# Target scores in fp32r, the x half of the output projection per group, destinations written by GpSimd, late gathers on two queues

## The reference, cut to what matters

```
q = (LN(x) @ Wtgt.T + b) * mask;  k, v = split((ctx @ Wsrc.T + b) * mask)     # 8 heads of 16
a = softmax(q @ k.T / 4, masked keys out) @ v
x = x + tanh(g0) * (concat[LN(x), a] @ Wout.T + b)          # Wout: 256 -> 128
p = softmax(LN(x) @ router.T);  two best of 8 experts, weights made to sum to 1
x = x + tanh(g1) * sum over the two of  w * (gelu(LN(x) @ w1[e]) @ w2[e])
```

## Time and profile before

| engine | busy us | share of the span | instructions |
|---|---|---|---|
| PE | 297.5 | 88% | 3633 |
| DVE | 212.3 | 63% | 905 |
| ACT | 189.1 | 56% | 470 |
| POOL | 205.9 | 61% | 274 |

### The profile page before, as it was taken

The page is one execution under the profiler, slowest core; times in us unless marked ns, Lnnn a source line. Parts: engine busy times, 40 slices in busy tenths (PEclk is TensorE's granted clock), DMA queues, the critical chain, the costliest instruction groups (busy, mean ns, idle before and its releaser), DMA issues.

```text
span 339.5 us, 10975 instructions
## 1 busy us (share of the span) xinstructions
PE 297.5 (88%) x3633; PEld 267.0 (79%) x3633; DVE 212.3 (63%) x905; ACT 189.1 (56%) x470; POOL 205.9 (61%) x274
## 2 busy tenths in 40 slices
PE   1989999999999999997989979999998999999500
PEld 1777777787877878785678969999998999999500
DVE  2457567679888887889677866338733343437720
ACT  3166758868696876767674437456444444444100
POOL 3433233243586867858367787878878865567821
PEclk9999999999999999999999989999999999999955
DMA  6524521213141211851244222211434432194451
GB/s 221 158 86 167 166 85 33 80 37 95 33 123 53 64 50 49 243 143 33 59 105 118 63 68 83 68 52 61 126 91 128 114 105 64 39 317 139 143 171 46
DMA packets 41236, 34.61 MB, mean 102 GB/s; under 512 B 5044, under 2 KB 36950, under 8 KB 41184
## 3 DMA queue, kind: packets, MB, share of 16 engines
q1 hardware_dynamic: 33152, 23.62, 24.6%
q0 software_dynamic: 4320, 8.47, 7.0%
q10 hardware_dynamic: 3712, 1.84, 1.9%
HBM read 22.35 MB, written 12.01 MB: 101 GB/s over the span
## 4 chain that ended last, share of the span: by engine, by line
PE 47%; POOL 21%; issue 13%; DVE 8%; ACT 4%; DMA 3%; SPq 1%; POOLq 0%; ACTq 0%; DVEq 0%
POOL rows L638 10%; PE ps_sc L1572 8%; POOL picked L656 8%; PE ps_o L1531 4%; PE ps_proj L1585 4%; PE ps_o L1585 4%; PE ps_proj L1460 3%; PE ps_proj L1463 3%; PE ps_sc L1413 3%; PE ps_sc L1425 3%; PE ps_sc L1408 2%; PE ps_xT L1454 2%; DVE rowmax L1205 2%; ACT xr L787 2%; POOL pscratch L651 2%
## 5 line engine op out<-in xcount | busy, mean ns | idle before, releaser
L656 POOL DMA_INDIRECT picked<-yo,xg x71 | 71.5, 1007 | 16.1 <-issue 11.1
L1572 PE MATMUL ps_sc<-xt,w1c 128*128 128x128 f32 x568 | 76.2, 278 | 3.2 <-issue 2.4
L638 POOL DMA_INDIRECT rows<-xr,posi x64 | 63.2, 987 | 18.0 <-issue 18.0
L1572 PEld LDWEIGHTS ps_sc<-xt,w1c 128*128 128x128 f32 x568 | 69.8, 194 | 4.3 <-issue 4.3
L821 ACT ACTIVATE probT<-ps_sc 128x512 f32<-128x512 f32 x71 | 42.4, 598 | 43.6 <-PE ps_sc L1572 43.6
L1205 DVE TENSOR_REDUCE rowmax<-ps_sc 128x4 f32<-128x512 f32 x64 | 43.7, 691 | 24.7 <-PE ps_sc L1429 20.6
L716 ACT ACTIVATE probT<-ps_sc,pencol 128x512 f32<-128x512 f32 x64 | 43.6, 683 | 20.5 <-PE ps_sc L1429 18.3
L586 POOL TENSOR_TENSOR kblk<-kT,headcol 128x256 f32<-128x256 f32 x32 | 19.7, 615 | 54.3 <-ACT kT L745 54.1
L1585 PE MATMUL ps_proj<-w2s,probT 128*128 x288 | 38.9, 279 | 0.0
L1585 PE MATMUL ps_o<-w2s,probT 128*128 x280 | 37.1, 275 | 0.0
L1323 DVE COPY w1c<-w1s 128x512 f32 x71 | 31.6, 449 | 7.1 <-PE ps_sc L1572 2.3
(11 more groups left out here) (166 smaller groups left out, 585.5 us busy)
## 6 DMA issues: line engine op xcount, KB each, us to landing
xg<-rows SPq DMA_DIRECT2D x71, 65.0 KB, 1.9
ctxs<-ctxT SPq DMA_DIRECT2D x32, 128.0 KB, 2.1
xs<-x SPq DMA_DIRECT2D x8, 256.0 KB, 3.3
maskbc<-mask SPq DMA_DIRECT2D x8, 256.0 KB, 4.0
w1s<-w SPq DMA_DIRECT2D x4, 512.0 KB, 3.6
w2s<-w SPq DMA_DIRECT2D x8, 256.0 KB
maskbc<-picked SPq DMA_DIRECT2D x4, 512.0 KB, 6.0
out<-xs ACTq DMA_DIRECT2D x6, 256.0 KB, 2.3
```

The costliest lines, as they stand in the source:

```text
L638: nc.gpsimd.indirect_dma_start(out=rows, out_offset=bass.IndirectOffsetOnAxis(ap=posi[:, i, pick, b:b + 1], axis=0), in_=xr[:, i, pick, b, ...
L656: nc.gpsimd.indirect_dma_start(out=picked, out_offset=bass.IndirectOffsetOnAxis(ap=xg[:, r, D + 1:D + 2].bitcast(I32), axis=0), in_=yo[:, ...
L1572: last = nc.tensor.matmul(ps_score[j % DEEP][:, c * 128:(c + 1) * 128], w1c[:, j % DEEP, c * 128:(c + 1) * 128], xt[:, j % XRING, :], star ...
```

## The change

- The target scores take fp32r operands: GpSimd makes a second product `kblkr`, ahead of `kblk`, and ScalarE a copy `qTr` of qT; TensorE waits for these, and for `kblk` only in the part of sequence m.
- The x half of the output projection leaves the step. `xnT` becomes a ring of 12, and at (G+3, 1) the group's four x halves are accumulated in `ps_tail` with the attention halves. DVE's add of the x half and `s_xo` go.
- 16 bf16 matmuls on a tile of ones at the start of TensorE's stream; DVE sets this tile first.
- GpSimd writes the destinations into `xr`, behind its waits for the group's scatter, and waits for its own write.
- Of the last seven sends the last two are again a pair.
- The late gathers 1 and 3 are issued by ScalarE, 0 and 2 by SyncE; both wait for the last 20 sends in the order of the slots; all late adds are DVE's.

```diff
@@ -60,6 +60,7 @@
 DEEP = 3
+WARM = 16
@@ -73,10 +74,12 @@
 KQ = 4
+XNRING = 3 * GROUP
 BOXES = 3
...
 SINGLY = SLOTS - 7
+LAST_PAIR = SLOTS - 2
@@ -218,10 +221,12 @@
         xn = sb("xn", [128, GROUP, D])
-        xnT = sb("xnT", [128, 2, T])
+        xnT = sb("xnT", [128, XNRING, T])
         kT = sb("kT", [128, KQ, T])
...
         kblk = sb("kblk", [128, KQ, PAIR, T])
+        kblkr = sb("kblkr", [128, KQ, PAIR, T], F32R)
+        qTr = sb("qTr", [128, KQ, T], F32R)
         spare = sb("spare", [128, 3 * GROUP * 2 * D])
@@ -409,11 +416,9 @@
-        ROUTE = 23
+        ROUTE = 22
@@ -556,13 +561,14 @@
-            for r in range(RING):
-                sp.wait_ge(f_send[r], 16 * len(range(r, SLOTS, RING)))
+            for j in range(SLOTS - RING, SLOTS):
+                sp.wait_ge(f_send[j % RING], 16 * (j // RING + 1))
             for i, (G, half) in enumerate(LATE):
-                sp.dma_start(yb[G][:, half], picked_v[:, late(G, half), :, :]).then_inc(s_late_yb[i], 16)
+                if not i % 2:
+                    sp.dma_start(yb[G][:, half], picked_v[:, late(G, half), :, :]).then_inc(s_late_yb[i], 16)
             for i, (G, half) in enumerate(LATE):
                 if i % 2:
-                    sp.wait_ge(s_pool_y2, i // 2 + 1)
+                    sp.wait_ge(s_late_y2, i + 1)
                     sp.dma_start(out_v[:, late(G, half), :], xs[:, late(G, half), :]).then_inc(s_out, 16)
@@ -583,6 +589,9 @@
                     wait(pool, s_sc, n - 2)
+                    nc.gpsimd.tensor_tensor(
+                        kblkr[:, r, :, :], kT[:, r, :].unsqueeze(1).broadcast_to([128, PAIR, T]),
+                        headcol[:, :].unsqueeze(2).broadcast_to([128, PAIR, T]), ALU.mult).then_inc(s_kblkr, 1)
                     nc.gpsimd.tensor_tensor(
@@ -632,6 +641,10 @@
                     pool.wait_ge(s_xr, G + 1)
+                    nc.gpsimd.tensor_copy(
+                        xr[:, i, :, :, D + 1].bitcast(I32),
+                        dest[:, bass.ds(GROUP * G, GROUP), :].rearrange("p b k -> p k b")).then_inc(s_label, 1)
+                    pool.wait_ge(s_label, G + 1)
                     settled()
@@ -665,23 +678,16 @@
                 j = slot_of(n, LAG_DOWN)
-                if j is not None and (j % 2 or j >= SINGLY):
+                if j is not None and (j % 2 if j < SINGLY else j != LAST_PAIR):
                     pool.wait_ge(f_y, j + 1)
-                    wait(pool, f_settled, j // 2 if j < SINGLY else SINGLY // 2 + j - SINGLY)
+                    wait(pool, f_settled, j // 2 if j < SINGLY else SINGLY // 2 + min(j, LAST_PAIR) - SINGLY)
                     settled().then_inc(f_settled, 1)
-                    if j < SINGLY:
+                    if j < SINGLY or j > LAST_PAIR:
                         send(j - 1)
...
             each_slot(step, slot)
-            for i, (G, half) in enumerate(LATE):
-                if i % 2:
-                    x2 = xs[:, late(G, half), :]
-                    pool.wait_ge(s_late_yb[i], 16)
-                    nc.gpsimd.tensor_tensor(x2, x2, yb[G][:, half, 0, :], ALU.add).then_inc(s_pool_y1, 1)
-                    pool.wait_ge(s_pool_y1, i // 2 + 1)
-                    nc.gpsimd.tensor_tensor(x2, x2, yb[G][:, half, 1, :], ALU.add).then_inc(s_pool_y2, 1)
@@ -722,8 +728,8 @@
                     act.wait_ge(s_xT, n + 1)
-                    wait(act, s_proj, n - 1)
-                    nc.scalar.activation(xnT[:, (k - LAG_PROJ) % 2, :], ps_xT[:, 0:T],
+                    wait(act, s_oproj, n // GROUP - 2)
+                    nc.scalar.activation(xnT[:, n % XNRING, :], ps_xT[:, 0:T],
                                          ACT.Copy).then_inc(s_xnT, 1)
@@ -732,6 +738,11 @@
                     exponent(n, FAR, far_heads, s_exp)
+                n = sequence(g, k, LAG_SCORE)
+                if n is not None:
+                    act.wait_ge(s_q, n + 1)
+                    wait(act, s_sc, n - 3)
+                    nc.scalar.activation(qTr[:, n % KQ, :], qT[:, n % KQ, :], ACT.Copy).then_inc(s_qr, 1)
                 G = group(g, LAG_ROUTE)
@@ -741,6 +752,7 @@
                     act.wait_ge(s_proj, n + 1)
+                    wait(act, s_kblkr, n - 3)
                     wait(act, s_kblk, n - 3)
@@ -829,9 +841,14 @@
                 store(G)
+            for j in range(SLOTS - RING, SLOTS):
+                act.wait_ge(f_send[j % RING], 16 * (j // RING + 1))
+            for i, (G, half) in enumerate(LATE):
+                if i % 2:
+                    act.dma_start(yb[G][:, half], picked_v[:, late(G, half), :, :]).then_inc(s_late_yb[i], 16)
             for i, (G, half) in enumerate(LATE):
                 if not i % 2:
-                    act.wait_ge(s_late_y2, i // 2 + 1)
+                    act.wait_ge(s_late_y2, i + 1)
                     act.dma_start(out_v[:, late(G, half), :], xs[:, late(G, half), :]).then_inc(s_out, 16)
@@ -862,6 +879,8 @@
                 nc.vector.tensor_scalar(ve[:, :], mv[:, :, 1], EPS, None, ALU.add).then_inc(done[1], 1)
+
+            nc.vector.memset(ones_b[:, :], 1.0).then_inc(s_ones, 1)
@@ -879,7 +898,6 @@
                                         ALU.add).then_inc(s_late, 1)
-                nc.vector.memset(ones_b[:, :], 1.0).then_inc(s_ones, 1)
                 nc.vector.tensor_reduce(
@@ -995,9 +1013,6 @@
                 wait(dve, s_send[box], SEND * used)
-                nc.vector.tensor_copy(
-                    xr[:, box, :, :, D + 1].bitcast(I32),
-                    dest[:, bass.ds(GROUP * G, GROUP), :].rearrange("p b k -> p k b")).then_inc(s_rt, 1)
                 dve.wait_ge(s_rt, ROUTE * G + 21)
@@ -1265,9 +1280,6 @@
                         ALU.add, ALU.mult).then_inc(s_q, 1)
-                    dve.wait_ge(s_xb, g)
-                    x1 = xs[:, bass.ds(n, 1), :].rearrange("p o d -> p (o d)")
-                    nc.vector.tensor_tensor(x1, ps_proj[:, 3 * T:4 * T], x1, ALU.add).then_inc(s_xo, 1)
                 G = group(g, LAG_ROUTE)
@@ -1280,7 +1292,7 @@
                     dve.wait_ge(s_oproj, G + 1)
-                    wait(dve, s_xo, GROUP * G + GROUP)
+                    dve.wait_ge(s_xb, G + 1)
                     x4 = xs[:, bass.ds(GROUP * G, GROUP), :]
@@ -1347,12 +1359,11 @@
             for i, (G, half) in enumerate(LATE):
-                if not i % 2:
-                    x2 = xs[:, late(G, half), :]
-                    dve.wait_ge(s_late_yb[i], 16)
-                    nc.vector.tensor_tensor(x2, x2, yb[G][:, half, 0, :], ALU.add).then_inc(s_late_y1, 1)
-                    dve.wait_ge(s_late_y1, i // 2 + 1)
-                    nc.vector.tensor_tensor(x2, x2, yb[G][:, half, 1, :], ALU.add).then_inc(s_late_y2, 1)
+                x2 = xs[:, late(G, half), :]
+                dve.wait_ge(s_late_yb[i], 16)
+                nc.vector.tensor_tensor(x2, x2, yb[G][:, half, 0, :], ALU.add).then_inc(s_late_y1, 1)
+                dve.wait_ge(s_late_y1, i + 1)
+                nc.vector.tensor_tensor(x2, x2, yb[G][:, half, 1, :], ALU.add).then_inc(s_late_y2, 1)
@@ -1369,6 +1380,10 @@
+            pe.wait_ge(s_ones, 1)
+            for i in range(WARM):
+                nc.tensor.matmul(ps_o[:, :], ones_b[:, :], ones_b[:, :].unsqueeze(1).broadcast_to([128, QUADS, 128]),
+                                 start=True, stop=True)
             pe.wait_ge(s_ident, 16)
@@ -1399,6 +1414,7 @@
                     pe.wait_ge(s_maxT, m + 1)
+                    pe.wait_ge(s_kblk, m + 1)
                     wait(pe, s_exp_near, m)
@@ -1415,14 +1431,12 @@
                 if n is not None:
-                    pe.wait_ge(s_kblk, n + 1)
-                    pe.wait_ge(s_q, n + 1)
-                    if n == 0:
-                        pe.wait_ge(s_ones, 1)
+                    pe.wait_ge(s_kblkr, n + 1)
+                    pe.wait_ge(s_qr, n + 1)
                     pe.wait_ge(s_pen, n // GROUP + 1)
...
                     for j, strip in enumerate(strips):
-                        nc.tensor.matmul(scores[:, j, TARGET], qT[strip, n % KQ, :], kblk[strip, n % KQ, :, :],
+                        nc.tensor.matmul(scores[:, j, TARGET], qTr[strip, n % KQ, :], kblkr[strip, n % KQ, :, :],
                                          start=m is None, stop=False, skip_group_check=True)
@@ -1455,7 +1469,7 @@
                     pe.wait_ge(s_ctx[b], 16 * g)
-                    wait(pe, s_xo, n)
+                    wait(pe, s_q, n)
                     for c in range(FCH):
@@ -1474,8 +1488,7 @@
                     pe.wait_ge(s_xnT, n + 1)
-                    nc.tensor.matmul(ps_proj[:, T:2 * T], wtgt, xnT[:, r, :], start=True, stop=True)
-                    nc.tensor.matmul(ps_proj[:, 3 * T:4 * T], xnT[:, r, :], wout_g[:, 0, :],
+                    nc.tensor.matmul(ps_proj[:, T:2 * T], wtgt, xnT[:, n % XNRING, :],
                                      start=True, stop=True).then_inc(s_proj, 1)
@@ -1504,8 +1517,10 @@
                     for b in range(GROUP):
```

(14 more changed lines are left out.)

## The result

The changed kernel takes 341.13 us in the median of 20 runs (337.43 to 346.38), the kernel before 341.25 (339.82 to 343.1). The ratio is 0.9947 [0.9922, 0.9972]: 1.8 us faster, where 4.5 were forecast. Inside this small number two large ones nearly cancel. "Ahead" and "behind" compare the starts of the same TensorE instruction in the two profiles.

A forecast was written before the change was run, and what follows sets the result against it. TensorE was taken to bound the kernel nearly everywhere, with GpSimd next. Slot 0 gains 4.2 us, the 42nd slot loses 1.2, the tail gains 1.5: 4.5 off 341.26 gives 336.8 us, range 334.0 to 340.0.

The forecast's parts named there:

- fp32r: Target scores in the attention loop: 0.22 us less a step, from 0.43; bounds 0 and 0.32.
- Out projection, the steps' lengths: Attention loop: steps k=0 to k=3 of 5.79, 5.26, 4.37, 3.93 us; a group 19.35, 0.36 less.
- that ring: k=3 steps: scores, exponent, maximum, reciprocal and `on`, PV, scores again, also over ScalarE and DVE; 4.15 to 3.93 us.
- The lead at (5,3): TensorE ahead of the kernel before at group 5, step k=3, from start and loop gains: 5.7 us.
- Start: First steps, with TensorE at full speed after the warm-up matmuls: 4.0 us less; lower bound 1.5, still cold.
- the clock is not kept: Rival: TensorE idles after the warm-up, so the start gains 1.5 us, not 4.0: 339.3 us; 13 in 100.
- What GpSimd pays: Second product 0.62 us a step, destinations' copy 0.4 a group: 2.9 more a group, 20.4 against TensorE's 19.35.
- Nobody feels this in the loop.: GpSimd's lag, some 3.4 us at (8,0), delays nothing in the attention loop: kblk made at 101.90 is read at 109.19.
- GpSimd takes over: Rival: products cost over 0.62 us, gain gone from 0.92; at 1.24 the time is 346 us; 9 in 100.
- slot 0: First expert slot, waiting for group 3's last rows: lead 6.8 less GpSimd's 2.6, so 4.2 us earlier.
- the 42nd slot: Expert slot waiting for group 7's last rows: three destination copies of 0.4 ahead of it lose 1.2 us.
- Tail: End of the kernel: settle 0.4, waits 0.55, gathers 0.4, adds 0.15; together 1.5 us less, bounds 0.6 to 2.5.

The follow-up runs named there:

- both ends: Kernel before with only the 16 warm-up matmuls and early memset, and the changed tail; loop as before: 335.87 us, ratio 0.983.
- the two pairs of runs above: Changed kernel, GpSimd reordered: 0.9872; also without tw, groups 5-7 destinations on DVE: 0.9851. Changed kernel, fp32 target scores: 0.9894; also all destinations on DVE: 0.9875.
- the 1x1 add: Changed kernel with one 1x1 add on GpSimd behind the last late add, read by nobody: 346.71 us, ratio 1.0103.

## Why the prediction was wrong, step by step

Seen as a ladder, by the ratios to the kernel before: both ends -5.8; with the accumulated projection -4.3; with the destinations on GpSimd -3.6; with fp32r and the second product, which is the change, -1.8. With fp32r for all scores and one product it is -11.2. The steps of 0.7 and less are not told from nothing.

**fp32r.** Right, near the upper bound: L1439 takes 0.12 on the chain for 0.43, 0.31 saved where 0.22 were taken.

**Out projection, the steps' lengths.** From (4,3): 6.03, 5.18, 4.29, 4.12, against 5.79, 5.26, 4.37, 3.93 forecast. k=1 and k=2 were right. k=0 lost 0.09 where 0.15 was to be gained (one group earlier it gained 0.13). k=3 gained 0.03 where 0.22 was, so the saving of fp32r does not shorten that ring. The two groups up to (5,3) gained 0.30 and 0.09 instead of 0.36 each. The lead at (5,3), 5.43, still came near the forecast of 5.7 (4.0 and 0.9, 0.1, twice 0.36), since its parts, 3.55 and 1.0, 0.5, 0.4, err both ways.

**Start.** Right for this pair of profiles: four pieces at 0.45 from the first, first maximum at 13.77, 3.55 ahead at (1,3). As a term of the median it holds only for a start that stays slow without it, and the warm-up does not secure it: in the eight other profiles with both warm-up and fp32r the lead at (1,3) is 1.4 to 3.6, and in six of them the clock falls back to the lower level at 16 to 17.5 us. So the rival "the clock is not kept" came true there in part.

```profile
7.98 0.45 PE ps_proj L1477 x4
...
13.77 0.69 DVE rowmax L1220
...
20.38 0.12 PE ps_sc L1439 x4
```

**What GpSimd pays.** This step failed: "Nobody feels this in the loop." The price of a product was right (0.62), and TensorE never waits for kblkr, but the step counted GpSimd's work as a length of its own queue and asked only who waits for its results. DVE is held beside its instructions. The rival "GpSimd takes over" let 0.62 pass as harmless and began to lose at 0.92; it was decided by where GpSimd's queue puts the bias add. GpSimd's added work, at the forecast price, put it 0.8 to 1.8 later in the step (the second product alone 1.2 to 1.5), and that was enough, through `tw`, `on` and TensorE's clock. Cost: 10.1 us of lead; slot 0 was to come 4.2 earlier and came 4.65 later. Before the 42nd slot 1.2 more were lost, as forecast. Of that the three destination copies explain some 0.9 (0.3 each, with the wait), and the two pairs of runs above that differ in them, among other things, gain 0.7 each, which is not told from nothing.

**Tail.** Mis-sized: 1.5 forecast, 6.5 measured in the two profiles. The parts that were listed make 1.7: settle 0.4, waits 0.1 (0.55 forecast), gathers and adds 1.2 (0.55 forecast). The rest, 4.8, is the end of the program, which before waited for GpSimd's end behind its last add; SyncE's wait of 5.0 stood in the trace, and the prediction stopped at the store. It didn't belong to the bounds of any term, and it alone is why the change was not slower: in the profiles, 5.86 late at the 42nd slot and 6.5 gained behind it.

**The range.** The median lies 1 us over its upper end. That it came so near is luck: in the profiles two errors of opposite sign, 8.9 at slot 0 and 5.1 in the tail, turn 4.5 into 0.7.

What stays open: which of DVE's instructions are held was not mapped by itself, nor why DVE gets in behind a product and not between the bias add and the product; and whether the order in GpSimd's queue could keep two products harmless was tried twice and not settled.

## What to carry to other kernels

Price added work on GpSimd by its neighbours too, and also by what it pushes later in GpSimd's queue: list the DVE instructions that read only SBUF and will lie beside it in time, and who stands behind them in DVE's queue; a short one in front of a critical one is enough. Follow the chain to the program's last instruction, not to the last store: an engine's own end can be the longest item of a tail. And judge a stretch's granted clock together with its waits: here another 3.2 us were lost at half speed behind a wait of 1.8.

## What the runs showed of the hardware that was not expected

- DVE instructions on SBUF (128x4 tensor_tensor; 128x2 tensor_scalar) were held beside GpSimd's; GpSimd's own took 0.62 as ever. Where the Trainium skill, "SBUF — State Buffer", section "Who interferes with whom", speaks of the lock for one whole instruction, here a single DVE instruction was held over two, the bias add and the product behind it (2.34 us in the run with the second product alone), and got in as the third began, although GpSimd made no gap.
- A program did not end until some 7 us after GpSimd's last instruction: 7.1 after its last add in the kernel before, and 7.1 after the 1x1 add, with waits of SyncE of 5.0 and 5.3.
- After the wait of 1.82 us TensorE ran at the lower level from 99.6 to 106.4, although it was busy without a gap; after one of 1.05, at (7,0), the stretch's granted clock stayed at 1.00.
